# A fused two-layer graph network: the gates' weights begin 32 bytes further on in on-chip memory

## The reference

```python
h = relu(layernorm(x))                      # layer 0
x = x + relu((D A D) @ h @ W.T + b)         # D A D: the normalised adjacency
h = relu(layernorm(x))                      # layer 1
x_conv = relu(bn2(conv17(relu(bn1(conv1(h))))) + h)
A = exp(-dist(s, s)) * adj                  # s = h @ w_se.T + b_se
x_nmp = A @ relu(h @ w_msg.T + b_msg)
gi = concat(x_conv, x_nmp) @ w_ih.T + b_ih  # 512 -> 768
gh = h @ w_hh.T + b_hh                      # 256 -> 768
r, z = sigmoid(gi_r + gh_r), sigmoid(gi_z + gh_z)
out = x + (1 - z) * tanh(gi_n + r * gh_n) + z * h
```

## The kernel before

| matmuls | columns | stationary operand | moving operand |
|---|---|---|---|
| gates, `P<-xnx/nmx/xcx,wg` | 512 | wg 256 | xnx, nmx, xcx 256 |
| gates, the last ones | 256 | wg 256 | 256 |
| frequencies, `P<-wh,xh` | 256 | xh 256 | wh 256 |
| `P<-ax,ms` | 256 | ms 256 | ax 256 |
| `P<-w1m,xx` | 512 | xx 352 | w1m 384 |
| `P<-w0,ag` | 256 | ag 352 | w0 384 |
| `P<-xx,wse` | 256 | wse 384 | xx 352 |

## Time and profile before

### The profile page before, as it was taken

The page is one execution under the profiler, slowest core; times in us unless marked ns, Lnnn a source line. Parts: engine busy times, 40 slices in busy tenths (PEclk is TensorE's granted clock), DMA queues, the critical chain, the costliest instruction groups (busy, mean ns, idle before and its releaser), DMA issues.

```text
span 1774.7 us, 30896 instructions
## 1 busy us (share of the span) xinstructions
PE 1760.4 (99%) x10778; PEld 1556.1 (88%) x10778; DVE 1199.4 (68%) x2318; ACT 998.8 (56%) x1787; POOL 815.6 (46%) x988
## 2 busy tenths in 40 slices
PE   8999999999999999999999999999999999999998
PEld 7999999999999989999988888888888888888887
DVE  8999999999999956655664544544545545445445
ACT  6888888888888866665742333332333323333322
POOL 5788888888777637655731221211221212212211
PEclk9999999999999999999999999999999999999999
DMA  6567676766666554444674345444345453454442
GB/s 221 176 201 213 201 211 202 213 201 204 193 195 192 156 163 156 161 174 157 234 221 103 72 106 125 93 110 107 78 114 118 91 119 76 102 120 98 104 96 42
DMA packets 531865, 262.70 MB, mean 148 GB/s; under 512 B 366215, under 2 KB 494471, under 8 KB 531710
## 3 DMA queue, kind: packets, MB, share of 16 engines
q1 hardware_dynamic: 531166, 260.66, 53.6%
q10 hardware_dynamic: 544, 0.07, 0.0%
HBM read 151.58 MB, written 109.05 MB: 147 GB/s over the span
## 4 chain that ended last, share of the span: by engine, by line
PE 96%; issue 1%; DVE 1%; POOL 1%; ACT 1%; DMA 0%; POOLq 0%; ACTq 0%; DVEq 0%
PE P L111 73%; PE P L612 6%; PE P L1019 4%; PE P L871 4%; PE P L641 4%; PE P L703 3%; PE P L660 2%; PE P L621 1%; POOL axl L575 0%; POOL af L572 0%; DMA x<-in_x 0%; DVE agl L417 0%; DVE xct L1033 0%; DVE sm L483 0%; DVE sm L515 0%
## 5 line engine op out<-in xcount | busy, mean ns | idle before, releaser
L998 POOL TENSOR_TENSOR xnx1l<-xnf,xnx1h 128x1024 fp32r<-128x1024 f32 x16 | 44.3, 2771 | 393.2 <-ACT xnx1h L991 393.2
L998 POOL TENSOR_TENSOR xnx0l<-xnf,xnx0h 128x1024 fp32r<-128x1024 f32 x15 | 40.9, 2729 | 273.4 <-ACT xnx0h L991 273.4
L1124 ACT ACTIVATE nn<-gn,col 128x512 f32<-128x512 f32 x64 | 46.4, 725 | 192.0 <-DVE gn L1145 192.0
L1121 ACT ACTIVATE tr<-P,cold 128x512 f32<-128x512 f32 x64 | 44.2, 690 | 179.8 <-PE P L111 179.8
L1141 DVE SCALAR_TENSOR_TENSOR gn<-tr,gn 128x512 f32<-128x512 f32 x64 | 44.1, 689 | 137.1 <-ACT tr L1121 137.1
L572 POOL TENSOR_TENSOR af<-af,at 128x512 f32<-128x512 f32 x64 | 110.1, 1720 | 42.9 <-ACT af L363 40.5
L575 POOL TENSOR_TENSOR axl<-af,axh 128x512 fp32r<-128x512 f32 x64 | 101.1, 1580 | 55.6 <-ACT axh L381 55.6
L612 PE MATMUL P<-ah,hd 128*128 128x256 f32 x512 | 122.6, 383 | 0.6 <-ACT hd L397 0.6
L1154 DVE SCALAR_TENSOR_TENSOR tz<-tz,tr 128x512 f32<-128x512 f32 x63 | 43.6, 693 | 109.3 <-ACT tz L1135 109.2
L1135 ACT ACTIVATE tz<-P,cold 128x512 f32<-128x512 f32 x63 | 43.4, 689 | 123.0 <-PE P L111 123.0
L111 PE MATMUL P<-w1mh,xxh 128*128 128x512 f32 x256 | 107.8, 421 | 0.0
(11 more groups left out here) (214 smaller groups left out, 6398.3 us busy)
## 6 DMA issues: line engine op xcount, KB each, us to landing
xh_d<-xst SPq DMA_DIRECT2D x64, 320.0 KB, 4.8
y_d<-yo SPq DMA_DIRECT2D x80, 256.0 KB, 2.0
yt<-y_d SPq DMA_DIRECT2D x128, 160.0 KB, 4.5
xl<-xh_d SPq DMA_DIRECT2D x36, 512.0 KB, 4.5
x<-in_x SPq DMA_DIRECT2D x64, 256.0 KB, 2.7
a<-in_adj SPq DMA_DIRECT2D x64, 256.0 KB, 3.0
at<-in_adjt SPq DMA_DIRECT2D x64, 256.0 KB, 4.2
x_d<-x SPq DMA_DIRECT2D x64, 256.0 KB, 4.4
```

The source lines that it names most:

```text
L998: e.e.tensor_tensor(o[1][:, :, :], xnf[p % 2][:, :, :, :].rearrange("p c i t -> p c (i t)"), o[0][:, :, :], ALU.subtract).then_inc(done, 1)
```

## The change

The start of `wg` moves up by 32 bytes, from 256 to 288 modulo 512. No other tile moves: `third` is made anew right behind, and `keep` isn't touched. The two halves now end 36,896 bytes from the start of `taps`, inside the 37,888 that `taps` takes, so nothing new is overlaid. No instruction is added, removed or put elsewhere, and no wait changes.

```diff
         third = Place(nc, keep.at)
         taps = keep("taps", [119, NW, 256])
+        third.at += 32
         wg = third.hl("wg", [128, 6, 768])
 
         third = Place(nc, keep.at)
```

## The result

| | before | changed |
|---|---|---|
| median, 4 runs each | 1776.2 us (1775.77 to 1776.61) | 1798.2 us (1797.76 to 1799.12) |
| ratio, 95% interval | | 1.0125 [1.0112, 1.0137] |
| the profiled execution | 1776.52 us | 1799.12 us |
| its span | 1774.7 us | 1797.3 us |

The changed kernel is slower by 1.25%, 22 us.

The account below looks back on a forecast made before the run. PE alone was taken to bound the third stage. Settled gate matmuls +21.9 us and narrow ones -0.1 us made +21.8 us, 1797.7 on the median 1775.95, called 1798; range 1765 to 1804 us.

Parts of the forecast that it names:

- What bounds the kernel: Third stage: the chain of waits is PE alone, so each nanosecond on a gate matmul's step is in the time.
- Step 1: Third stage, 3,319 settled 512-column gate matmuls: step from 226.7 to 233.3 ns, +6.6 ns each, +21.9 us.
- Don't settle: Claim that matmuls with operands 32 bytes apart never reach the constant step, staying at 233 ns instead of 226.7.
- Step 2: Unsettled gate matmuls, 17 x 7, already at 232 ns: costed at nothing, at most 2 ns each, 0.2 us.
- Step 3: The 36 narrow gate matmuls of the last product: step from 120 to 117 ns, -0.1 us.
- Steps 4 and 5: DVE copies that write wg, taken as 0 (at most 0.2 us); and nothing coming late next in the third stage.
- First rival: Wide gate matmuls take the narrow families' gain: 1767 us at 224 ns, 1754 at 220; chance 0.22.
- the weak point: In the analogy to the first stage's wide family: no 512-column row had the stationary operand 32 bytes above the moving one.
- Second rival: Gate matmuls unchanged: offset modulo 64 doesn't matter, P<-w1m,xx is slow for its own reason; 1776 us, chance 0.16.
- Third rival: Gate matmuls in a worse state than P<-w1m,xx, up to 236 ns or more: +31 us, 1807 us, chance 0.04.

Follow-up runs that it names:

- both288: Against the kernel before, the gates' weights and all their moving halves 32 bytes further on, both at 288 modulo 512, distance 0: 1776.46 us.
- mov288: Against the kernel before, only the gates' moving halves 32 bytes further on, at 288, weights still at 256, distance -32: 1798.66 us.
- xx384: Against the kernel before, the first stage's xx moved from 352 to 384, level with w1m: 1775.21 us against 1776.37, ratio 0.9993.
- the run with all three shifts: Against the kernel before, xx and ax in the first stage and wh in the second each shifted 32 bytes: 1771.77 us, ratio 0.9973; the faster kernel.

## Why the prediction was right

The forecast was 1798 us; 1798.2 was measured.

- **What bounds the kernel** (PE alone in the third stage): right. 22.1 of the 22.6 us between the spans are between the starts of gate matmuls, so what the steps gained came through to the time.
- **Step 1, +6.6 ns on 3,319 settled matmuls, +21.9 us**: right in size, 226.8 to 233.3 over all, 22.1 us by the starts of the gate matmuls. The reason given, that operands at equal offsets settle and others don't, is borne out for the gates by both288 and mov288: what counts is the distance, and not where the weights lie. Two things in it were luck. The offsets were compared modulo 64, and that is wrong: at a distance of 64, equal modulo 64, the step is 233.3 as well. At a distance of 32 both ways of comparing say the same, apart. And P<-w1m,xx, whose 233 ns were the price, isn't slow by its own distance alone: made level by itself (xx384) its steps behind the first fall only from 232.9 to 230.3 on average, and to 227.1 when ax is moved too (the run with all three shifts).
- **"Don't settle"** is too simple. The steps fall into a pattern there too (236, 231, 236, 231 at +64; 235, 234, 231, 238, 237, 231, 234 at +96), only not into a constant one.
- **Step 2, the unsettled ones at nothing**: right within its 2 ns. Over all runs the second to the sixth step go from 231.6 to 232.8 ns. In the row behind an idft they were at 232 and are at 234, from the second to the seventh matmul:

```profile
1064.79 0.40 PE L111 MATMUL P<-xnx1l,wgh 128*128 128x512 f32 x1
...
1065.96 0.40 PE L111 MATMUL P<-xnx1h,wgh 128*128 128x512 f32 x1
```

- **Step 3, narrow ones from 120 to 117**: right in sign, 118.2, -0.06 us of the -0.1. The rows of the last 24, answering to the earlier trace rows, 2.72 us over 23 steps:

```profile
1789.17 0.28 PE L111 MATMUL P<-xcx1h,wgh 128*128 128x256 f32 x1
...
1791.89 0.28 PE L111 MATMUL P<-xcx1h,wgl 128*128 128x256 f32 x1
```

- **Steps 4 and 5, nothing**: right. The last four subtractions that write wg take 3.56 us in both kernels, and no new wait of PE is in the third stage: the only one is for xcx0l, 0.3 us before and 0.2 now.
- **First rival** (the wide matmuls take the narrow ones' gain): wrong at every distance that was tried; no mean wide step fell below 226.8 ns. The sign of the distance, called the weak point, doesn't count at 32 bytes, but may further out: +64 has 233.3, and +192, which is -64 if the period is 256, has 229.1.
- **Second rival** (no change): out. The rule of the Trainium skill beside it (TensorE: Matmul & The Clock Gate, Step-by-step: what each phase is for) has the two read ports as independent and a weight load as taking no read bandwidth from the running matmul. What the prediction drew from it, no change, the runs don't bear out: the same gate matmuls take from 226.8 to 234.3 ns by nothing but the distance between the two operands. Whether it is the weight load that meets the running matmul, no run shows.
- **Third rival** (a worse state, 236 ns and 1807 us): not here. The worst that was seen is 234.3 ns and 1802.1 us, at +96.

Why the distance counts isn't shown. That the streaming of one matmul and the loading of the next one's weights meet in memory would fit a step that depends on the distance between both addresses, and records that grow with the step (389 to 396 ns); no run took the weight load away from beside the matmul. Also open is why narrow matmuls prefer another distance than wide ones.

## What to carry to other kernels

Where a profile shows the matrix engine without a gap and its steps are still longer than columns over clock, read the starts of single matmuls, tabulate the step by family against both operands' offsets, and let the families that differ price a layout before it is tried. In this kernel the wide gate matmuls were shortest with both operands level modulo 256 bytes, and narrow ones with them apart, by 32 to 96 or by 192 bytes; at 128 there was no gain. A gain of that kind on one engine is worth only what the next one can follow: of some 7 us (net) saved on PE's steps in the first two stages, 2.8 went into a wait for the vector engine.

## What was not expected of the hardware

- The step of these fp32r gate matmuls in a row depends on the distance between the two operands' offsets: for 512 columns 226.8 ns at 0, 256 and 512, 232.4 to 234.3 at +-32, 64, 96 and 128, 229.1 at 192. A period of 256 bytes fits all of these.
- For 256 columns the order is another (35 steps in one execution each): 113.3 ns at 192, 116.7 to 118.6 at +-32, 64 and 96, 119.8 and 120.0 at 0 and 128. The narrow families of the first two stages at a distance of 192 weren't tried; 6.5 ns a step is over twice what the faster kernel takes from them.
- The distance of its own two operands doesn't settle a family's step alone: the wide family of the first stage, level in both kernels, reaches 227 ns at its tenth matmul when xx alone was moved, and at its second when ax (and, in the second stage, wh) was moved as well. The second stage runs later, so what differs ahead of these matmuls is the move of ax, with that of the tiles behind it by 512 bytes. That a state carries over from the matmuls before would explain it; no run shows what carries it.
